# Cross-attention stage of a two-layer kernel: five engine programs in a new order with a period of four units, numerators weighted before the denominators are inverted, row normalisation moved to ScalarE

## The reference, cut to what matters

```python
x = x + _L0_ffn_ref(_layernorm(x), ...)
# _L1_xattn_ref(_layernorm(x), ctx): 16 heads of 32 features, linear attention
q = query @ Wq.T                      # [4, 512, 512]
gate = sigmoid(query @ Wg.T + bg)
q = where(q > 0, q + 1, exp(q))       # feature map
kv_summary = einsum('bhsd,bhse->bhde', k, v); k_sum = k.sum(-2)
z = 1.0 / (einsum('bhld,bhd->bhl', q, k_sum) + 1e-6)
attn = einsum('bhld,bhde->bhle', q, kv_summary) * z
x = x + (attn * gate) @ Wo.T
x = x + _L1_ffn_ref(_layernorm(x), gate_w, ...)   # router: softmax(x @ gate_w.T), top 4 of 16
```

## Time and profile before

| what | value |
|---|---|
| median of 3 runs | 1075.52 us (1074.67 to 1082.87) |
| profiled execution, device time | 1072.68 us |
| profiled execution, span of the trace | 1071.0 us |
| PE busy | 1027.2 us (96%) |
| DVE, ACT, POOL busy | 687.5, 620.6, 349.2 us |
| PE's share of the chain that ended last | 64% |

### The profile page before, as it was taken

One profiled execution on the slowest core, in us unless ns is written; L12 is line 12 of the kernel. 1 busy time (PEld: TensorE's weight loads), 2 busy tenths in 40 slices (PEclk: granted clock), 3 DMA queues, 4 the chain that ended last, 5 costly groups with the idle time before them and its releaser, 6 DMA issues.

```text
span 1071.0 us, 15883 instructions
## 1 busy us (share of the span) xinstructions
PE 1027.2 (96%) x5555; PEld 797.6 (74%) x5578; DVE 687.5 (64%) x1227; ACT 620.6 (58%) x938; POOL 349.2 (33%) x500
## 2 busy tenths in 40 slices
PE   9999999999999999788998979999999999999996
PEld 6888888884555555556776657888888899999996
DVE  7767555368999897366665564668742666666662
ACT  5876887747999888754344423511112566666662
POOL 1023223055555541433233324400010044444442
PEclk9999999999999999899998889999999999999998
DMA  6684666422100001201211115320232678888863
GB/s 237 238 307 132 188 197 177 129 59 80 31 21 21 21 11 40 69 1 49 89 50 59 40 66 160 93 81 11 69 111 89 224 227 238 237 239 239 238 160 50
DMA packets 47970, 127.93 MB, mean 119 GB/s; under 512 B 6176, under 2 KB 6176, under 8 KB 47136
## 3 DMA queue, kind: packets, MB, share of 16 engines
q1 hardware_dynamic: 36880, 98.49, 27.6%
q0 software_dynamic: 10448, 27.53, 11.0%
q10 hardware_dynamic: 576, 1.05, 0.3%
HBM read 98.74 MB, written 28.31 MB: 119 GB/s over the span
## 4 chain that ended last, share of the span: by engine, by line
PE 64%; DVE 5%; ACT 3%; POOL 2%; issue 2%; DMA 0%; SPq 0%; POOLq 0%; DVEq 0%; ACTq 0%
PE bank L60 15%; PE bank L61 14%; PE bank L62 14%; PE bank L1576 8%; PE bank L1597 4%; PE bank L2466 1%; PE bank L1650 1%; PE bank L1649 1%; PE bank L1588 1%; DVE a_th L1927 1%; PE bank L1606 1%; DVE f_sg L1915 1%; ACT f_sg L1332 0%; ACT f_sg L1330 0%; PE bank L1669 0%
## 5 line engine op out<-in xcount | busy, mean ns | idle before, releaser
L1576 PE MATMUL bank<-w,f_qT 128*128 128x512 bf16 x496 | 115.9, 379 | 2.1 <-DVE f_h L1855 1.0
L2288 POOL DMA_INDIRECT out<-e_y,scatter_idx x32 | 69.0, 2157 | 109.5 <-ACT e_y L2395 89.6
L1576 PEld LDWEIGHTS bank<-w,f_qT 128*128 128x128 bf16 x512 | 48.6, 98 | 51.7 <-issue 1.3
L2271 POOL DMA_INDIRECT e_xg<-xn_rows,gather_idx x32 | 32.1, 1004 | 162.1 <-DVE gather_idx L2674 96.5
L2326 ACT ACTIVATE s_m_h<-s_mid 128x512 fp32r<-128x512 f32 (+1 forms) x24 | 15.2, 632 | 106.5 <-DVE s_mid L2684 60.6
L1597 PE MATMUL bank<-w,f_q2T 128*128 128x512 bf16 x249 | 57.3, 379 | 0.7 <-ACT f_q2T L1302 0.3
L2792 DVE TENSOR_TENSOR e_mid<-bank,e_sil 128x256 f32<-128x256 f32 (+1 forms) x47 | 19.8, 420 | 59.2 <-ACT e_sil L2365 59.2
L60 PE MATMUL bank<-e_xT_h,e_wg_h 128*128 128x256 f32 (+1 forms) x192 | 55.1, 287 | 0.0
L1855 DVE SCALAR_TENSOR_TENSOR f_h<-bank,f_columns,f_sg 128x512 f32<-128x512 f32 x64 | 47.9, 749 | 11.1 <-PE bank L1576 6.2
L61 PE MATMUL bank<-e_xT_l,e_wu_h 128*128 128x256 f32 (+1 forms) x192 | 54.1, 282 | 0.0
L62 PE MATMUL bank<-e_xT_h,e_wu_l 128*128 128x256 f32 (+1 forms) x192 | 54.0, 281 | 0.0
(11 more groups left out here) (468 smaller groups left out, 3346.0 us busy)
## 6 DMA issues: line engine op xcount, KB each, us to landing
wraw<-in_wffn SPq DMA_DIRECT2D x48, 512.0 KB, 4.5
e_raw_g<-in_ew_gate SPq DMA_DIRECT2D x16, 704.0 KB, 4.2
e_raw_u<-in_ew_up SPq DMA_DIRECT2D x16, 704.0 KB, 5.5
e_raw_d<-in_ew_down SPq DMA_DIRECT2D x16, 512.0 KB, 6.6
sorted_y<-e_y SPq DMA_DIRECT2D x19, 256.0 KB, 4.1
x_rows<-rows SPq DMA_DIRECT2D x16, 256.0 KB, 2.0
xn_rows<-a_work SPq DMA_DIRECT2D x16, 256.0 KB, 2.0
s_raw<-x_rows SPq DMA_DIRECT2D x16, 256.0 KB, 2.7
```

Source lines behind the costliest of these rows:

```text
L1576: ins = pe.matmul(bank[c % 2][:, :], qT[t % 2][:, k * P:(k + 1) * P], w_gv(k, col + c * 512), start=(k == 0), stop=(k == KD - 1))
L2271: gp.indirect_dma_start(xg[t][u][:, :], None, g.xn_dram, bass.IndirectOffsetOnAxis(g.gather_idx[:, slot:slot + 1], 0)).then_inc(e_arrived[ ...
L2288: gp.indirect_dma_start(io["out"], bass.IndirectOffsetOnAxis(g.scatter_idx[:, slot:slot + 1], 0), e_y[t][u][:, :], None, compute_op=ALU.ad ...
```

## The change

- `attend(n)` waits for `weighted` of the unit before and for its denominators' copies, no longer for `att_ready`. A new DVE step `weigh_numerators(n)` computes (th + 1) times the numerators straight from the banks, in place in th, in two halves; the multiplication with the inverted denominators, one instruction, comes last in `attended`.
- `a_normalise(s)` is an ACTIVATE on ScalarE with scale and bias from POOL, which computes one more small operation in `row_scale(s)` (the shift) and has two sets of these columns.
- The first four queries go to the banks 2, 1, 4, 5; gate(0) no longer waits, attend(0) waits for fewer of them. Each later query waits for the bank that it needs. From row tile 12 on the odd projections go to a second bank.
- The tables are gone. The order repeats with four units: projections and turns of the batch before, two or more queries of the batch after.
- Batch 0's logits are made by `route_batch` and `turn_logits` too. At the edge to the shared expert the order of pieces, loads and row tiles is new.
- On POOL, low_query(0) and low_query(1) come ahead of `after(15)`.

```diff
+                    if i == TT + 1:
+                        gp.wait_ge(shift2_ready, TT - 1)
+                        low_query(0)
+                        low_query(1)
                     if have(i - 2):
                         after(i - 2)
...
                 def attend(n):
...
                     if n:
-                        pe.wait_ge(att_ready, n)
+                        pe.wait_ge(weighted, n)
+                        pe.wait_ge(den_ready, 2 * n)
                     else:
-                        pe.wait_ge(feature_ready, CT + KD)
+                        pe.wait_ge(feature_ready, CT + 2)
...
+                def weigh_numerators(n):
+                    v.wait_ge(th_ready, n + 1)
+                    v.wait_ge(n_ready, 2 * n + 2)
+                    v.scalar_tensor_tensor(out=th[UPPER, :], in0=th[UPPER, :], scalar=1.0, in1=nbank[0][UPPER, :], op0=ALU.add, op1=ALU.mult)
+                    v.scalar_tensor_tensor(out=th[LOWER, :], in0=th[LOWER, :], scalar=1.0, in1=nbank[1][LOWER, :], op0=ALU.add, op1=ALU.mult).then_inc(weighted, 1)
...
-                    v.scalar_tensor_tensor(out=th[:, :], in0=th[:, :], scalar=1.0, in1=den, op0=ALU.add, op1=ALU.mult).then_inc(weight_ready, 1)
...
-                    v.tensor_tensor(att[UPPER, :], nbank[0][UPPER, :], th[UPPER, :], ALU.mult)
-                    v.tensor_tensor(att[LOWER, :], nbank[1][LOWER, :], th[LOWER, :], ALU.mult).then_inc(att_ready, 1)
+                    v.tensor_tensor(att[:, :], th[:, :], den, ALU.mult).then_inc(att_ready, 1)
...
+                def a_normalise(s):
+                    act.wait_ge(arstd_ready, 2 * s + 2)
+                    if s >= 2:
+                        act.wait_ge(xn_out[s % 2], 16 * (s // 2))
+                    act.activation(a_xn[s % 2], g.rows[:, s, :], ACT.Identity, bias=a_shift[s % 2], scale=a_rstd[s % 2]).then_inc(xn_ready, 1)
```

The new order on PE, in its own words (before = first tile of the batch before, then = first unit of the batch after):

```diff
                 for n in range(TT):
                     attend(n)
+                    if b == 0:
                         gate(n + 1)
+                        query(n + KD)
+                        if n == 1:
+                            turn_x(TT - 1)
+                    elif c == 0:
+                        project(before)
+                        gate(n + 1)
+                        project(before + 1)
+                        if b > 1:
+                            turn_logits(b - 2)
+                    elif c == 1:
+                        a_turn_x(before)
+                        project(before + 2)
+                        gate(n + 1)
+                        project(before + 3)
+                        a_turn_x(before + 1)
+                    elif c == 2:
+                        if then < TT:
+                            query(then)
+                        a_turn_x(before + 2)
+                        gate(n + 1)
+                        if then < TT:
+                            query(then + 1)
+                        a_turn_x(before + 3)
+                    else:
+                        if then < TT:
+                            query(then + 2)
+                            gate(n + 1)
+                            query(then + 3)
+                        route_batch(b - 1)
+                pe.wait_ge(feature_ready, CT + TT)
+                shared["expand"](0, 0, (0,))
+                pe.wait_ge(weighted, TT)
+                pe.wait_ge(den_ready, 2 * TT)
+                shared["expand"](0, 0, (1,))
+                project(EARLY)
+                project(EARLY + 1)
```

323 lines of the change are left out of this document (175 added, 148 removed).

## The result

| what | before | after |
|---|---|---|
| median of the runs timed together | 1078.01 us (1074.67 to 1082.87) | 1042.03 us (1041.28 to 1042.94) |
| ratio, 95% interval | | 0.9663, 0.9619 to 0.9707 |
| profiled execution, device time | 1072.68 us | 1041.57 us |
| profiled execution, span | 1071.0 us | 1039.5 us |

The change made the kernel 36.0 us faster by the medians and 31.1 us by the profiled pair. The two differ because the profiled execution of before is faster than the four runs timed beside it, which scatter by 8 us. The forecast was 28.6 us less, 1047 us, within its range of 1037 to 1061.

The account below looks back on a forecast made before the run. The prediction took PE's waits (30.4 us) and low clock (14.3 us), from order and latency, as the bound. It took off 18.8 of waits, 8.5 of low clock and 1.3 of router: 28.6 us less, 1047 us, range 1037 to 1061.

Parts of the forecast that it names:

- gate(1) for tanh(0): At the stage's start, PE waits 4.1 us because gate(1) writes the bank that tanh(0) reads.
- gate(4) for tanh(3): In the units without projections, unit 2's split of the last feed-forward tile delays `att`: 1.3 us of wait at gate(4).
- turn of tile 10: Behind attend(14), a_turn_x(10) waits 2.1 us for tile 9's split on DVE, which stands behind two new instructions.
- route_batch(2): Behind attend(15), it waits 2.15 us for the split of tile 11.
- batch 1's summaries: Fetched once attend(3) is done, 7.4 us to attend(4) against 6.9 of PE work: 0.5 us of wait.
- projections for the sums: Projections waiting for the residual sum of the tile before: 1.1 us allowed in all, against 4.4 before.
- rival B: Loops longer than laid out: stretched last multiplication, 7 us more waits, clock falling as before; 1062, or 1055 at half; chance 0.17.
- The low clock: In the attention stage, time lost at 1.2 GHz falls from 14.3 to 5.8 us, 8.5 us less.
- the router: Four routes become eight matmuls of 512 columns and four small turns: 1.3 us saved.
- A: Rival: the clock stays up after the start, waits 9 us and low clock 1.3; 35.7 us less, 1040 us; chance 0.17.
- C: Rival: late weight pieces at the hand-over make PE wait and nearly all is lost, 1070 us; chance 0.05.
- D: Rival: the serial loop through th, every stage stretched, reaches 12.7 us per unit; 12 us slower, 1088; chance 0.03.

Follow-up runs that it names:

- low queries late: The changed kernel with POOL's low parts of queries 0 and 1 again behind the last tile's steps: 1045.28 us, ratio 0.9718.
- start alone: The kernel before with only the new start (first queries' banks and waits, POOL's low parts of queries 0 and 1 earlier): 1074.81 us, ratio 0.9979.
- formula alone: The kernel before with only the new formula, attend waiting for weighted numerators and the denominators' copies: 1076.26 us, ratio 0.9996.
- the gate between: The kernel before with, in units of two projections, the first made ahead of the next unit's gate: 1076.67 us, ratio 0.9999.
- the queries ahead: The kernel before with only its table of queries changed, queries 10, 11 and 13 to 15 coming earlier: 1067.14 us, ratio 0.9913.
- the last kernel: The changed kernel with tanh(0), unit 0's denominators and weighing earlier, unit 2's split behind tanh(3), and two fills of nine unread matmuls: 1034.82 us, ratio 0.9600.
- no late splits: The changed kernel with unit 2's feed-forward split behind tanh(3), and the end's turns and route_batch one step later: 1045.80 us, ratio 0.9703.
- tanh(0) first: The changed kernel with tanh(0) on ACT ahead of the last tile's normalisation and query 3's features: 1040.24 us, ratio 0.9651.

## Why the prediction was right

**The direction and the mechanism held**: what PE waited for is gone, and little new came in its place. The forecast was 5 us above the median. Against the sum's own profile, 28.6 us were forecast and 31.1 measured.

**The waits**: 11.6 us forecast, 11.4 measured. Term by term:

| term | forecast | measured |
|---|---|---|
| gate(1) for tanh(0) | 4.1 | 4.22 |
| gate(4) for tanh(3) | 1.3 | 1.37 |
| turn of tile 10 | 2.1 | 2.36 |
| route_batch(2) | 2.15 | 2.36 |
| a route for its logits copy | 0.35 | 0.38 |
| batch 1's summaries | 0.5 | none |
| projections for the sums | 1.1 | none |
| gate(0) for the low part of wg | not foreseen | 0.68 |

The total agrees better than its terms: 1.6 us that did not come are made up by 0.7 us not foreseen and 0.7 us more in the others, which is luck. Of the two that did not come, the wait for sums was an allowance on a layout that had 0.6 to 1.3 us to spare, and the one for the summaries was laid out as a wait of 0.5 us and was wrong. The first row, too, is near for a reason that the prediction didn't have: attend(0) ended at 447.74 and tanh(0) at 451.91, each 1.0 or 1.1 us later than laid out. The one not foreseen is in the timeline of the start: DVE's four subtractions for wg took 4.08 us where they had taken 2.47 before, and POOL's second low part, which now runs beside them, 1.62 instead of about 1.28. The same stretch holds up phi(2)'s step on DVE until 444.91, and with it tanh(0). With the low parts back behind (low queries late) the wait was gone, and in the kernel with the start alone the 4.08 came again. This is what "SBUF — State Buffer" of the Trainium skill (section "Who interferes with whom") states: a VectorE instruction with two SBUF inputs contends with a GpSimd one that reads SBUF. The trace agrees, with 4.08 against 2.47 us on DVE and 1.62 against 1.28 on POOL. The prediction had weighed that rule for the attention's multiplication, and not at the one place where the change moved POOL's work beside DVE's.

**Loops (rival B)**. The last multiplication, the transpositions' successor, was as long as line 1927; instructions of the line, ns shortest, median and longest:

```profile
L1999 DVE TENSOR_TENSOR a_att<-a_th,a_work x16: 691/693/1601, 455.1 to 608.0; 128x512 f32<-128x512 f32 x16
```

It was stretched in 4 of the 16 units (to 1.60, 1.46, 1.00 and 1.01 us), which is less than B's half, and no unit from 4 to 13 waits. B was right that it is stretched and wrong on how often and on what hangs on it. The experiment with the formula alone shows where the same loop costs 5.5 us.

**The low clock**: 8.5 us less were forecast. After, the excess over the undisturbed durations is 2.4 us in gate(1), 482.21 − 477.85 − 2.86 = 1.5 in gate(4), and 1.6 and 1.5 behind the two waits at the end, 7.0 us where 5.8 were forecast; all three later places fell, where two had been counted. Before, the same reading of the groups gives 3.0 us in unit 0 with the turn ahead of it, 1.5 in the units 3 and 4, 1.5 in unit 11, 3.0 in unit 12, 3.0 in unit 14, and 2.2 in attend(15) and the projection behind it: 14.2, where 14.3 had been priced from unit 12 alone. So 7.2 came off. "TensorE: Matmul & The Clock Gate" of the Trainium skill (section "HAM oscillation — how this bites in real kernels") prices time at the lower clock at half of itself: by that, 17 us would be 8.5, an estimate by the page, against 7.0 read here. The measurement decides.

**The term that was missed**: a wait costs more than the idle time that is read. In the timeline above, a matmul starts at 442.76, and the next at 443.83 behind 0.68 us of idle. Undisturbed the distance is 0.23, so 1.07 − 0.23 = 0.84 us were lost. The other 0.16 us is the modelled end of the record, which overlaps the next start in a running row of matmuls; the first distance behind the wait, 0.34, is 0.11 longer again. Over the 17 waits above 0.3 us before, the loss over the idle time adds up to about 3.9 us, and over the 6 of after to 0.6. That is some 3.3 us more that the change gave back, a tenth of its gain, and the largest part of what the forecast was short of.

**The whole**, read over PE's groups from the stage's start to the shared expert's first contraction: 19.0 us of waits, 3.3 of this, 7.2 of low clock and 1.2 in the router (0.5 by the groups' times, which hold 0.7 us of low clock after; 1.3 forecast): 30.7 of 31.5. The other 0.8 us I can't place.

**What the parts are worth.** Alone, on before: the formula 0, the gate's place 0, the start 2.7, the queries ahead 9.4, and these with the formula 13.9 us. Taken back from after: the formula 2.4, the normalisation 0, POOL's low parts at the start 3.2. The parts alone sum to 12, with the formula on top of the queries to some 17, and the whole gave 36. Between them lies the order on DVE, ACT and PE of projections, sums, turns and splits, which was run only as a whole: what it is worth by piece stays open. The one edit of before that moved nothing but PE's program, the gate between, gave nothing.

**The other rivals.** A had the clock up after the start, and it fell three more times; the last kernel comes near it by fills, with one fall left. C needed a late piece at the hand-over, and the expert's groups wait for none, with 1.0 us to spare at the first; in the kernel with no late splits it came true there, by 5.0 us. D needed gates or attends that wait in the units 4 to 13, and there are none.

**My expectations** were worst where one cause was to be removed and the next one behind it was not priced: the formula alone (6 to 11 expected, 0 to 1 measured), the queries ahead (12 to 18, 9.4), the gate between (3 to 6, 0 to 1), tanh(0) first (5, 1.8) and no late splits (4 to 9 faster, 3.8 slower).

## What to carry to other kernels

Find the loop that closes behind the one you cut, and count the work of the waiting engine that lies in it: the same new formula was worth 0 us in an order with no group of matmuls between attend and gate, and the new order without it already 33 us. Look at what the late result stood behind on its own engine, and at what that waited for: moving only the projection and the gate of the waiting engine left the wait for sums as it was. Where a wait on TensorE can't be removed, unread matmuls in it kept the clock up here: worth 2.4 us for one wait of 4.2 us.

## What the runs showed of the hardware that I had not expected

- Behind a wait, TensorE loses about 0.16 us more than the idle time in the record when a matmul of a gate, query or projection stands ahead of the wait. The first distance between starts behind it was 0.34 us instead of 0.23 in the gate above (443.83 to 444.17), but 0.23 in the batch's logits (606.47 to 606.70), at the full clock.
- The length of a wait does not by itself decide whether the clock falls. In the last kernel, a wait of 2.08 us had no fall behind it and one of 1.46 us had: the first distance behind it is 0.33 us in the one and 0.59 in the other.

```profile
465.67 0.50 PE L60 MATMUL bank<-xT_h,a_wg_h 128*128 128x512 f32 x1 [2.08 <-ACT a_th L1368]
466.00 0.39 PE L61 MATMUL bank<-xT_l,a_wg_h 128*128 128x512 f32 x1
...
481.56 0.80 PE L60 MATMUL bank<-a_wo_h,a_q_first 128*128 128x512 f32 x1 [1.46 <-POOL a_q_first L1218]
482.15 0.63 PE L61 MATMUL bank<-a_wo_l,a_q_first 128*128 128x512 f32 x1
```

- attend is slowed less by the lower clock than gate is: before, attend(12) and attend(15) took 2.70 and 2.87 us against 1.70, and in after gate(1) took 5.28 against 2.86. So where a fall lands changes what it costs.
